# Three head tiles of every late attention step exponentiated on GpSimd as powers of a constant, and the late steps regrouped

## What is computed

```python
x = L0_attn_x
xn = _layernorm(x, axis=-1)
# attention: q, k, v = heads(xn @ W.T), rotary turn of q and k, then
attn = jnp.einsum('bhnd,bhmd->bhnm', q, k) * scale      # scale = 8 ** -0.5
attn = jax.nn.softmax(attn, axis=-1)
out = jnp.einsum('bhnm,bhmd->bhnd', attn, v)
# experts: two best of softmax(xn @ gate_w + gate_b), each a gelu MLP of three layers
x = x + attention(xn) + ffn(xn)
```

## Time and profile before

| what | us |
|---|---|
| median of 2 runs | 640.43 (640.36 to 640.51) |
| the profiled execution, its own time | 641.5 |
| its span, first to last instruction | 639.8 |
| ScalarE busy | 546.8 |
| TensorE busy | 599.6 |
| VectorE busy | 239.1 |
| GpSimd busy | 166.9 |

### The profile page before, as it was taken

One profiled execution on the slowest core, in us unless ns is written; L12 is line 12 of the kernel. 1 busy time (PEld: TensorE's weight loads), 2 busy tenths in 40 slices (PEclk: granted clock), 3 DMA queues, 4 the chain that ended last, 5 costly groups with the idle time before them and its releaser, 6 DMA issues.

```text
span 639.8 us, 12291 instructions
## 1 busy us (share of the span) xinstructions
PE 599.6 (94%) x4152; PEld 260.1 (41%) x4152; DVE 239.1 (37%) x742; ACT 546.8 (85%) x555; POOL 166.9 (26%) x187
## 2 busy tenths in 40 slices
PE   9889999999999998998999999999898998999895
PEld 6323332222222222222999999982222222222221
DVE  5655224766352335022565556630202020211204
ACT  3799999999999998999555555569999999999994
POOL 2700000001444444531122221223332333323310
PEclk9999999999999999999999999999999999999999
DMA  7654611532464246783333333311212111121204
GB/s 226 182 181 163 233 34 50 198 138 99 149 210 149 91 140 227 246 260 82 81 76 74 74 74 74 74 37 42 71 44 69 58 58 57 62 77 42 71 13 135
DMA packets 82625, 70.74 MB, mean 111 GB/s; under 512 B 44288, under 2 KB 58400, under 8 KB 82576
## 3 DMA queue, kind: packets, MB, share of 16 engines
q1 hardware_dynamic: 76000, 56.34, 29.1%
q0 software_dynamic: 5856, 13.05, 6.6%
q10 hardware_dynamic: 720, 0.71, 0.5%
HBM read 32.92 MB, written 32.96 MB: 103 GB/s over the span
## 4 chain that ended last, share of the span: by engine, by line
PE 62%; ACT 17%; issue 12%; DMA 3%; DVE 3%; SPq 1%; POOL 1%; DVEq 1%; ACTq 0%; POOLq 0%
PE ps L1411 18%; ACT probs L663 15%; PE ps L1394 11%; PE ps L1343 10%; PE ps L1335 5%; PE ps L1356 5%; PE ps L1318 3%; PE ps L1262 2%; ACT probs L641 2%; DMA k_st<-k_d 2%; DMA work<-slots_y_d,slot_i 2%; PE ps L1298 2%; PE ps L1225 1%; PE ps L1196 1%; DVE x_all L1133 1%
## 5 line engine op out<-in xcount | busy, mean ns | idle before, releaser
L663 ACT ACTIVATE probs<-ps 128x1536 f32<-128x1536 f32 (+1 forms) x308 | 408.6, 1432 | 8.2 <-PE ps L1394 6.6
L1411 PE MATMUL ps<-probs,v_st 128*32 128x512 f32 x1792 | 238.7, 604 | 4.4 <-DVE v_st L789 3.2
L1394 PE MATMUL ps<-q_st,k_st 32*128 32x512 f32 x896 | 154.5, 494 | 22.4 <-ACT probs L663 18.3
L1394 PEld LDWEIGHTS ps<-q_st,k_st 32*128 32x128 f32 x896 | 57.9, 181 | 235.0 <-ACT probs L663 172.7
L677 ACT ACTIVATE work<-ps,work 128x256 f32<-128x256 f32 (+1 forms) x156 | 64.9, 455 | 60.4 <-PE ps L1343 60.2
L541 POOL DMA_INDIRECT slots_x_d<-xn_all,slot_i x64 | 62.9, 983 | 196.9 <-DVE expert_i L987 127.2
L579 POOL DMA_INDIRECT work<-slots_y_d,slot_i x64 | 60.6, 947 | 122.0 <-PE ps L1411 79.2
L1343 PE MATMUL ps<-work 128*128 128x256 f32 (+1 forms) x312 | 68.0, 361 | 0.0
L641 ACT ACTIVATE probs<-ps 128x1024 f32<-128x1024 f32 x64 | 60.6, 1034 | 3.7 <-PE ps L1298 2.7
L1411 PEld LDWEIGHTS ps<-probs,v_st 128*32 128x32 f32 x1792 | 35.6, 107 | 60.7 <-issue 54.5
L789 DVE COPY v_st<-v_all 128x128 f32<-128x128 f32 (+1 forms) x32 | 8.5, 265 | 131.3 <-PE ps L1411 131.3
(11 more groups left out here) (177 smaller groups left out, 379.0 us busy)
## 6 DMA issues: line engine op xcount, KB each, us to landing
k_d<-parts SPq DMA_DIRECT2D x8, 1024.0 KB, 5.7
q_d<-parts SPq DMA_DIRECT2D x8, 1024.0 KB
q_st<-q_d SPq DMA_DIRECT2D x30, 256.0 KB
k_st<-k_d SPq DMA_DIRECT2D x30, 256.0 KB
slots_x_d<-parts SPq DMA_DIRECT2D x5, 1024.0 KB, 7.4
work<-slots_x_d SPq DMA_DIRECT2D x128, 32.0 KB, 1.9
slots_y_d<-work POOLq DMA_DIRECT2D x32, 128.0 KB, 2.2
work<-work SPq DMA_DIRECT2D x24, 128.0 KB
```

Source lines behind the costliest of these rows:

```text
L663: nc.scalar.activation(group_probs(phase, g)[:, 0:size, :], group_slot(g)[:, 0:size * HALF].rearrange("p (h n) -> p h n", n=HALF), ACT.Exp ...
L1394: ins = nc.tensor.matmul(group_slot(g)[:, n * HALF:(n + 1) * HALF], k_st[32 * h:32 * h + ROWS, mt * P:(mt + 1) * P], q_st[32 * h:32 * h + ...
L1411: ins = nc.tensor.matmul(o_ps[32 * h:32 * h + 32, :], v_window(mt, h, half), group_probs(phase, half * HALF_GROUPS + g)[:, n, :], start=be ...
```

## The change

Per late step the 64 tiles are divided anew. Key block 0 of the second half of the queries is taken out. Of its 4 head tiles, 3 go to GpSimd and 1 to ScalarE alone; the other 60 tiles go to ScalarE in 20 groups of 3 (`LATE_ITEMS`), which now run over the border of the halves.

- TensorE makes the scores of the four tiles one by one into `aux_ps`, in slots 2 to 5 (`help_scores`), each after VectorE has copied the one before it out to `he_s` (`read_help`). ScalarE exponentiates the fourth straight from `aux_ps` behind its group 7.
- GpSimd raises a constant, exp(scale), to the power of the three scores in one instruction of 128 x 1536 elements (`help_exps`), in its queue behind the gathers of the first tile and ahead of those of the other four.
- The values of that block are multiplied in slot 17 (`help_values`), and `turn` moves to slot 9.
- On VectorE the copy of the next step's first values (`load_v(t + 1, 0)`) moves behind `combine`, `normalise` of the step before moves ahead of it, and `finish_rows` of the first three batches moves from the end of the program into steps 11, 13 and 14, between `combine` and `load_v`.
- SP's waits follow the new group numbers. The needed halves of `q_st` are now wanted in slot 2, not only at group 11. The loops over the late steps run over one step at a time, and on VectorE they are written out.

```diff
+LATE_ITEMS = [(0, mt, h) for mt in range(MT) for h in range(HG)] + [(1, mt, h) for mt in range(1, MT) for h in range(HG)]
+LATE_GROUPS = len(LATE_ITEMS) // 3
+LATE_BLOCKS = [(0, mt) for mt in range(MT)] + [(1, mt) for mt in range(1, MT)]
+HELP_AT = 2
+HELP_HEADS = (0, 3, 2, 1)
+HELP_VALUES = 17
+def late_sums(n):
+    return n + 1 + (late_ending(HELP_VALUES) <= n)
...
+        he_s = part(2 * GATHER * C, 3 * HALF)
...
+            return probs[:].rearrange("p a h n -> p (a h) n")[:, 3 * (g % GROUP_RING):3 * (g % GROUP_RING) + 3, :]
+        help_probs = probs[:, PROB_RING - 1]
...
+            def help_exps(i):
+                if i == 0:
+                    pool.wait_ge(S["base_made"], 1)
+                pool.wait_ge(S["help_read"], 3 * i + 3)
+                pool.wait_ge(S["pv_done"], (SPLIT + i) * BLOCKS + BLOCKS)
+                nc.gpsimd.tensor_tensor(help_probs[:, 1:HG, :].rearrange("p h n -> p (h n)"), exp_base[:].to_broadcast([P, 3 * HALF]), he_s,
+                                        ALU.pow).then_inc(S["help_made"], 1)
             for i in range(STEPS - SPLIT):
                 if i >= 1:
                     pool.wait_ge(S["combined"], i)
                 for k in range(min(GATHER, TILES - GATHER * i)):
+                    if k == 1:
+                        help_exps(i)
                     block_done((SPLIT + i) * BLOCKS + 3 * k)
...
-            group_exps(SPLIT, 1, True)
-            with act.Fori((SPLIT + 1) // 2, STEPS // 2) as i:
-                group_exps(i * 2, 0)
-                group_exps(i * 2 + 1, 1)
+            def late_exps(t, first=False):
+                for g in range(LATE_GROUPS):
+                    act.wait_ge(S["scores_done"], group_units(t) + (g + 1))
+                    if g >= GROUP_RING:
+                        act.wait_ge(S["pv_done"], t * BLOCKS + (BLOCKS + late_sums((3 * (g - GROUP_RING) + 2) // HG)))
+                    elif first:
+                        act.wait_ge(S["pv_done"], t * BLOCKS + BLOCKS)
+                    else:
+                        act.wait_ge(S["pv_done"], t * BLOCKS + late_sums((3 * (g - GROUP_RING + LATE_GROUPS) + 2) // HG))
+                    nc.scalar.activation(late_probs(g), group_slot(g).rearrange("p (h n) -> p h n", n=HALF),
+                                         ACT.Exp, scale=SCALE).then_inc(S["exp_done"], 1)
+                    if g == HELP_AT + 5:
+                        act.wait_ge(S["help_scored"], (t - SPLIT) * HG + HG)
+                        nc.scalar.activation(help_probs[:, 0, :], aux_ps, ACT.Exp, scale=SCALE).then_inc(S["help_exp"], 1)
+            late_exps(SPLIT, True)
+            with act.Fori(SPLIT + 1, STEPS) as t:
+                late_exps(t)
...
-            with dve.Fori(SPLIT, STEPS - 1) as t:
+            def read_help(t):
+                for k in range(3):
+                    dve.wait_ge(S["help_scored"], (t - SPLIT) * HG + k + 1)
+                    if k == 0 and t > SPLIT:
+                        dve.wait_ge(S["help_made"], t - SPLIT)
+                    nc.vector.tensor_copy(he_s[:, k * HALF:(k + 1) * HALF], aux_ps).then_inc(S["help_read"], 1)
+            finished = {11: 0, 13: 1, 14: 2}
+            dve.wait_ge(S["x_scattered"], 16 * 2 * TILES)
+            for t in range(SPLIT, STEPS - 1):
+                read_help(t)
+                if t > SPLIT:
+                    normalise(t - 1)
+                combine(t - SPLIT)
+                if t in finished:
+                    finish_rows(finished[t] * BT, BT).then_inc(S["out_ready"], 1)
                 load_v(t + 1, 0)
-                combine(t - SPLIT)
                 copy_o(t)
                 load_v(t + 1, 1)
-                normalise(t)
             last = STEPS - 1
+            read_help(last)
+            normalise(last - 1)
             copy_o(last, 0)
             normalise(last, (0,))
             combine(last - SPLIT, TILES - GATHER * (last - SPLIT))
-            dve.wait_ge(S["x_scattered"], 16 * 2 * TILES)
-            for b in range(B - 1):
-                finish_rows(b * BT, BT).then_inc(S["out_ready"], 1)
             finish_rows((B - 1) * BT, BT // 2).then_inc(S["out_ready"], 1)
             copy_o(last, 1)
...
+            def late_scores(t, g, first=False):
+                items = LATE_ITEMS[3 * g:3 * g + 3]
...
+            def help_scores(t, k):
+                if k == 0:
+                    pe.wait_ge(S["q1_loaded"], t * 16 + 16)
+                    free_aux(aux_of_turn(t - 1))
+                else:
+                    pe.wait_ge(S["help_read"], (t - SPLIT) * 3 + k)
+                h = HELP_HEADS[k]
+                nc.tensor.matmul(aux_ps, k_st[32 * h:32 * h + ROWS, 0:P], q_st[32 * h:32 * h + ROWS, HALF:N],
+                                 start=True, stop=True).then_inc(S["help_scored"], 1)
...
+            def help_values(t):
+                pe.wait_ge(S["help_exp"], t - (SPLIT - 1))
+                pe.wait_ge(S["help_made"], t - (SPLIT - 1))
+                for h in range(HG):
+                    ins = nc.tensor.matmul(o_ps[32 * h:32 * h + 32, :], v_window(0, h, 1), help_probs[:, (HELP_HEADS.index(h) + 1) % HG, :],
+                                           start=False, stop=False)
+                ins.then_inc(S["pv_done"], 1)
...
+            def late_step(t, first=False, last=False):
+                for g in range(LATE_GROUPS):
+                    if g < LATE_GROUPS - 1:
+                        late_scores(t, g + 1, first=(first and g == 0))
                     elif not last:
-                        group_scores(t + 1, 0)
+                        late_scores(t + 1, 0)
                     if first and g == 0:
                         pe.wait_ge(S["y_made"], SLOT_TILES + 2)
                     if first and g < 2:
                         for _ in range(WARM_LATE[g]):
                             nc.tensor.matmul(aux_ps[:, 0:HALF // 2], zeros[:, 0:P], zeros[:], start=True, stop=True)
-                    if isinstance(t, int) and t < SPLIT:
-                        if g in JOB_PLACE:
-                            extra_piece(t, JOB_PLACE[g])
-                    else:
-                        if g == 5 and not first:
-                            turn(t - 1)
-                        if g == HALF_GROUPS + 5 and last:
-                            turn(t, 0)
+                    if HELP_AT <= g < HELP_AT + HG:
+                        help_scores(t, g - HELP_AT)
+                    if g == HELP_AT + 7 and not first:
+                        turn(t - 1, 0, True)
+                    if g == 13 and last:
+                        turn(t, 0)
+                    if g == HELP_VALUES:
+                        help_values(t)
                     if g > 0:
-                        j = block_ending_in(g - 1)
-                        if j is not None:
-                            group_values(t, j, phase, apart=(last and t == STEPS - 1))
-                    elif not first and not joined:
-                        group_values(t - 1, BLOCKS - 1, 1 - phase)
+                        n = late_ending(g - 1)
+                        if n is not None:
+                            late_values(t, n, last)
+                    elif not first:
+                        late_values(t - 1, len(LATE_BLOCKS) - 1)
...```

In the rows below each line is one or more instructions in the order of the engine's program; the names are output<-inputs, and what stands in brackets are the semaphores that it waits for. First GpSimd's queue in a late step. `work` is the buffer in which `gath` and `he_s` lie, `probs` takes the exponentials. Before:

```order
L579 DMA work<-slots_y_d,slot_i 128x128 [waits pv_done,combined]
L579 DMA work<-slots_y_d,slot_i 128x128
L579 DMA work<-slots_y_d,slot_i 128x128 [waits pv_done]
L579 DMA work<-slots_y_d,slot_i 128x128
L579 DMA work<-slots_y_d,slot_i 128x128 [waits pv_done]
```

96 lines of the change are left out of this document (69 added, 27 removed).

## The result

| | before | after |
|---|---|---|
| median of 2 runs | 640.43 us | 2294.39 us (2293.80 to 2294.98) |
| ratio | 1 | 3.582, 95% interval 3.573 to 3.591 |
| span of the profiled execution | 639.8 us | 2293.3 us |
| granted TensorE clock, mean | 1.00 | 0.64 |

The changed kernel is three and a half times slower. The forecast was 658.1 us with a range up to 700. It had the direction and the loop right, and the length of one instruction, the power, wrong by a factor of twenty (244.5 us for 11.9).

The account below looks back on a forecast made before the run. The prediction took ScalarE to bound the kernel, with the chain of gathers, `combine` and copy also at the limit. It summed 640.4 + 15.6 (loop) + 3.4 - 1.3 to 658.1 us, range 635 to 700.

Parts of the forecast that it names:

- the loop: Once per late step: third copy, power, eight gathers, `combine`, `copy_o`, next first values; forecast 31.5 us against 28.9.
- What X is: Step pricing X, GpSimd's power over 1536 elements per partition: 11.9 us, with ends 3.8 and 19.8.
- The sum is 19.6 + X: Length of the loop between first values of successive steps: 19.6 us plus the power's time X.
- + 3.4: Cost of `finish_rows` standing on the loop in three steps, 1.14 us each: +3.4 us.
- - 1.3: ScalarE's saving, counted once after step 15's first values, where the loop is over: 28.4 - 27.1, -1.3 us.
- dear rival: Power on GpSimd above 16 us: 682 us at X = 16, 706 at 20; chance 0.20.
- cheap rival: Power below 9 us, so the chain from block 12 limits the step: 28.7 us, 641 in all; chance 0.25.
- six times -0.2: In the cheap rival, six late steps of 28.7 us, limited by the chain from block 12, each 0.2 us shorter.
- full gain: The chain of gathers has slack and ScalarE runs gapless at 27.1 us per step: -12.3 us, 628 us; chance 0.05.
- at most 1.8 us per step: ScalarE's saving in late steps from the new groups, 27.1 against 28.9 us, if nothing else is late.
- Single score tiles at nothing: TensorE's four single score tiles per late step cost nothing, covered by the group beside them; uncovered, up to 1.7 us.
- The second half's loads: Loads of `q_st`'s second half arrive before the single tile's slot: no wait, about a microsecond spare.

Follow-up runs that it names:

- e2: The changed kernel with GpSimd's power for one of the three tiles and a product for the other two; 1170.22 us.
- e1: The changed kernel with a product in place of GpSimd's power, so the three tiles hold no exponentials; 654.94 us.
- e9: e1 with `finish_rows` of the three early batches back at the end of the program, as in the kernel before; 651.25 us.
- e6: e1 with VectorE's copies of sum, next values and next step's single tiles all ahead of `combine` and `finish_rows`; 641.74 us.
- e11: e6 with the five pairs of gathers waiting for blocks 4, 7, 9, 12, 14 instead of 0, 3, 6, 9, 12; 635.16 us.
- e10: e6 without arithmetic on GpSimd: VectorE copies the three tiles' scores straight into `help_probs`, no exponentials; 648.89 us.
- e8: e6 with the three tiles' exponentials approximated by squarings on VectorE and that block's values one slot later; 633.39 us.

## Why the prediction was wrong

*The step that failed is "What X is".* It took a power for three passes of an addition's cost, 11.9 us, with 3.8 and 19.8 as ends. X is 244.5 us. An addition costs 1.27 us for 512 columns, 2.5 ns each, a power 159 ns, 64 times as much. No row bounded that from above, and the upper end was built from the same guess as the value: that a logarithm and an exponential cost a pass or two each. The Trainium skill (GPSIMD Engine Reference, Performance versus the Vector engine) gives 12 cycles per element for code that branches; the trace here has 159 ns, which is an estimated 191 cycles of the 1.2 GHz that the page gives. So neither the rows nor the page priced it, and I should have said that the rows give a lower bound only. The sum itself asked for it: the forecast hung on X alone (9.3 us no change, 11.1 measurable, 16 dear), and I gave the case above 16 a chance of 0.20 and the range an end at X = 19.

*The loop held.* "The sum is 19.6 + X" was measured at 21.5 + X in the full change (266.1 - 244.5) and in e2 (105.3 - 83.9), and 0.8 to 1.2 us longer where a `finish_rows` stands, for the 1.14 priced. With 244.5 for 11.9 my own sum gives: six rounds of 264.1 - 28.9, 1411 us; the seventh power, of which some 16 us were hidden before slot 17, 228; then + 3.4 and - 1.3: 640.4 + 1641 = 2282 us against 2294. Of the 12 us that are missing some 9.5 lie in the five rounds behind the first. The first, at full clock, took 263.8 us from first values to first values (431.89 to 695.69), as summed; the others took 266.1 to 267.3. The term that was short is the one from the first values to the next power, priced at 3.8 us: it took 3.84 in the first round (431.89 to 435.73) and 6.1 in the second (695.69 to 701.80), with values at 1.93 instead of 1.06 us and scores at 0.80 instead of 0.50, at a granted clock of 0.52. From `combine` to the first values the sum was 0.4 us too long. The last 3 us lie behind step 15's first values.

*The dear rival's sign was there*, the wait of slot 17 for `help_made`. Its price, 706 us, was for X = 20.

*The cheap rival* (641 us) is what e1 tried, and it came at 655. So my claim that an X below 9 makes no difference was wrong by 14 us too. Its term for `finish_rows`, +3.4, held (e9: 3.7). What failed is "six times -0.2": that chain was followed with the kernel before's gaps, 2.78 us from the last gather to `combine` (3.5 to 4.2 us in e1, 3.4 to 4.0 in e9, with loads issued beside it), and without the price of a wait on TensorE, which comes back at half clock. That VectorE's order was to blame for most of it, e6 shows (13 us under e1).

*The full gain* (27.1 us per step) was given 0.05. As a rival for the changed kernel it fell; but its step was shown in e11, 27.4 us with ScalarE gapless. ScalarE's price, "at most 1.8 us per step", held: 28.9 - 27.4 is 1.5.

*Single score tiles at nothing*: right. In e1 and after it each starts within 0.2 us of the group's scores (517.99 and 518.18 in e1), and the values follow 0.42 us later as before. *The second half's loads*: no wait of a slot for them was seen, but they stand beside the last gather in e1, whose landing came later; I had not priced that.

## What to carry to other kernels

A bound by the nearest rows holds only for the same kind of work: for an elementary function on GpSimd that no row shows, additions bound it from below only, and it should be measured on a small tile before a plan is built on it. When an engine's queue feeds a loop through other engines, write down the loop as a constant plus the unknown; here that sum was within 1% at a value twenty times the one assumed. And order counts as much as work: the same instructions ran in 655, 642 and 635 us by where the copies stood on VectorE and how far apart the gathers were. And when a row names a releaser whose work had long ended, look at when the semaphore was counted up before calling the row wrong.

## What the hardware did that I had not expected

- A GpSimd power costs 159 ns per column, independent of exponents and of the number of partitions (1, 16, 128: 10.51 us for 64 columns). Six squarings of all three tiles on VectorE take 10.7 us.
- ScalarE stands still for 1.3 to 2.0 us behind six gathers that go out 1.25 us apart (e6, e10). At 1.79 us apart (e8) this was not seen, and in pairs (e11) once. TensorE's semaphores are counted up late then, by up to 2.9 us in e6, in one bunch with 11 to 16 counts of the gathers' landings (5 in e11), though its matmuls had run. What holds the counts up is open.
- A gather's issue takes 1.49 us beside VectorE's squarings and 1.81 beside `finish_rows` (e1, 520.46 beside 520.23), 0.95 alone.
- After a wait of TensorE of 1.88 us its clock was at half level in the slots that followed (e9, wait before 554.24: scores 0.80 us instead of 0.50 at 555.25); after one of 1.67 us it stayed full (e6, wait before 511.00).
